# The last pass over each down weight piece on GpSimd instead of ScalarE

## The reference

```
scale = cond @ norm_w.T + 1.0
h = x * (scale[:, None, :] * rsqrt(mean(x * x, -1) + 1e-6))
val, gate = split(h @ up_w.T, 2, axis=-1)
h = val * gelu(gate)
hq = clip(round(h * s), -128, 127) / s        # s = 127 / max|h| of the token
wq = clip(round(down_w * t), -1, 1) / t       # t = 1 / mean|down_w|, one number for all
y = hq @ wq.T + x
```

## Time and profile before

| | |
|---|---|
| device time, median of 3 runs | 810.25 us (809.88 to 810.6) |
| profiled execution, its span (the page gives no other time of it) | 807.4 us |
| TensorE busy | 772.0 us, 96% |
| VectorE busy | 605.6 us, 75% |
| ScalarE busy | 443.2 us, 55% |
| GpSimd busy | 255.6 us, 32% |
| ScalarE's last pass over a down piece (L655), 8 times | 1.05 us each (median) |
| GpSimd's passes L527 and L530 over a down piece, 8 times each | 1.12 and 1.22 us each (medians) |

### The profile page before, as it was taken

One profiled execution on the slowest core, in us unless ns is written; L12 is line 12 of the kernel. 1 busy time (PEld: TensorE's weight loads), 2 busy tenths in 40 slices (PEclk: granted clock), 3 DMA queues, 4 the chain that ended last, 5 costly groups with the idle time before them and its releaser, 6 DMA issues.

```text
span 807.4 us, 18034 instructions
## 1 busy us (share of the span) xinstructions
PE 772.0 (96%) x6401; PEld 635.0 (79%) x6401; DVE 605.6 (75%) x852; ACT 443.2 (55%) x1025; POOL 255.6 (32%) x318
## 2 busy tenths in 40 slices
PE   5898988999799999999999999999999999999998
PEld 4687877788688877897788877898788877888753
DVE  5987987799568973899558973898558973887367
ACT  5687767587566643555446643555446643554323
POOL 3875966354422321123212321122212321111021
PEclk9999999999999999999999999999999999999999
DMA  5485764876465554654565554654565545555432
GB/s 207 169 264 170 239 226 175 309 243 218 160 223 198 185 187 148 223 206 145 188 213 200 184 169 151 230 203 140 193 219 195 182 162 162 188 187 175 133 126 83
DMA packets 37963, 152.90 MB, mean 189 GB/s; under 512 B 3608, under 2 KB 4128, under 8 KB 37920
## 3 DMA queue, kind: packets, MB, share of 16 engines
q1 hardware_dynamic: 37376, 152.06, 55.5%
q10 hardware_dynamic: 544, 0.27, 0.1%
HBM read 130.16 MB, written 22.15 MB: 189 GB/s over the span
## 4 chain that ended last, share of the span: by engine, by line
PE 71%; DVE 7%; DMA 1%; issue 1%; ACT 1%; SPq 0%; DVEq 0%; ACTq 0%
PE Y L1142 11%; PE A L1091 11%; PE A L1094 11%; PE A L1093 11%; PE B L1091 8%; PE B L1094 8%; PE B L1093 8%; DVE h L872 2%; DMA wslots<-w_scratch 1%; DVE h L838 1%; PE X L1039 1%; DVE h L832 1%; DVE mpart L851 1%; PE X L1131 1%; DVE q L877 1%
## 5 line engine op out<-in xcount | busy, mean ns | idle before, releaser
L1091 PE MATMUL A<-xT,wslots 128*128 (+1 forms) x1024 | 280.9, 274 | 13.4 <-ACT snapC L616 9.1
L1093 PE MATMUL A<-xT,wslots 128*128 (+1 forms) x1024 | 280.9, 274 | 0.0
L1094 PE MATMUL A<-xT,wslots 128*128 (+1 forms) x1024 | 280.9, 274 | 0.0
L509 POOL TENSOR_TENSOR snapC<-snapC 128x256 f32<-128x256 f32 x128 | 100.5, 785 | 503.4 <-ACT snapC L616 503.3
L1091 PE MATMUL B<-xT,wslots 128*128 (+1 forms) x768 | 210.4, 274 | 2.1 <-DVE h L832 2.1
L1093 PE MATMUL B<-xT,wslots 128*128 (+1 forms) x768 | 210.3, 274 | 0.0
L1094 PE MATMUL B<-xT,wslots 128*128 (+1 forms) x768 | 210.2, 274 | 0.0
L838 DVE SCALAR_TENSOR_TENSOR h<-h,c_all,g 128x512 f32<-128x512 f32 (+1 forms) x128 | 103.7, 810 | 111.0 <-ACT g L639 110.7
L1091 PEld LDWEIGHTS A<-xT,wslots 128*128 128x128 f16 x1024 | 100.7, 98 | 30.3 <-ACT snapC L616 11.0
L1093 PEld LDWEIGHTS A<-xT,wslots 128*128 128x128 f16 x1024 | 100.7, 98 | 14.6
L1094 PEld LDWEIGHTS A<-xT,wslots 128*128 128x128 f16 x1024 | 100.8, 98 | 12.2
(11 more groups left out here) (137 smaller groups left out, 944.0 us busy)
## 6 DMA issues: line engine op xcount, KB each, us to landing
wslots<-w_scratch SPq DMA_DIRECT2D x105, 896.0 KB, 4.6
w_scratch<-wslots SPq DMA_DIRECT2D x15, 896.0 KB, 5.2
wst<-in_L_cond_up_w_dram SPq DMA_DIRECT2D x16, 512.0 KB, 6.5
xin<-in_x_dram SPq DMA_DIRECT2D x8, 1024.0 KB, 7.5
dwb<-in_L_cond_down_w_dram SPq DMA_DIRECT2D x16, 512.0 KB, 4.4
wst<-in_x_dram SPq DMA_DIRECT2D x28, 256.0 KB, 5.3
out_dram<-wst SPq DMA_DIRECT2D x28, 256.0 KB, 2.1
xin<-in_x_dram SPq DMA_DIRECT2D x4, 256.0 KB, 4.1
```

Source lines behind the costliest of these rows:

```text
L509: pool.tensor_tensor(snapC[:, s % 2, 0:H], snapC[:, s % 2, 0:H], snapC[:, s % 2, H:T], ALU.add)\
L1091: pe.matmul(into, high, xh, start=(start and kp == 0), stop=False, skip_group_check=not start)
L1093: pe.matmul(into, high, xl, start=False, stop=False, skip_group_check=not start)
L1094: mm = pe.matmul(into, low, xh, start=False, stop=last, skip_group_check=not start)
```

## The change

GpSimd makes the third pass itself, right behind its second, in down_clip, with a tensor_scalar (subtract MAGIC, multiply by 1.0) that writes f16 into tern. The two waits of the pass go with it. ScalarE's down_round and its table of slots are gone. The signal dw_rounded now comes from GpSimd; the transposes of TensorE and the loads of SyncE wait for it as before, and stand where they stood.

```diff
--- before.py
+++ after.py
@@ -109,7 +109,6 @@
     PC = FF // 2
     DW_SUM = {2 * i: i for i in range(PIECES)}
     DW_CLIP = {s: i for i, s in enumerate((0, 2, 3, 5, 6, 9, 11, 13))}
-    DW_TERN = {s + 1: i for s, i in DW_CLIP.items()}
     DW_T = {s + 2: i for s, i in DW_CLIP.items()}
     DW_LOAD_WITH = {6: 3, 7: 4, 9: 5, 10: 6, 13: 7}
 
@@ -529,6 +528,10 @@
                 pool.wait_ge(dw_added, i + 1)
                 pool.tensor_scalar(dwb[:, i % 2, :], dwb[:, i % 2, :], MAGIC + 1.0, MAGIC - 1.0, ALU.min, ALU.max)\
                     .then_inc(dw_clipped, 1)
+                pool.wait_ge(dw_clipped, i + 1)
+                at_least(pool, dT_psum, i - 1)
+                pool.tensor_scalar(tern[:, i % 2, :], dwb[:, i % 2, :], MAGIC, 1.0, ALU.subtract, ALU.mult)\
+                    .then_inc(dw_rounded, 1)
 
             def batch(b, first=False, final=False):
                 for s in range(FT):
@@ -649,11 +652,6 @@
                 act.activation(q_of(LAST, i), h_tiles(LAST, 2 * PAIR_ORDER[i], 2), ACT.Copy, bias=-MAGIC)\
                     .then_inc(qe_rounded_act, 1)
 
-            def down_round(i):
-                act.wait_ge(dw_clipped, i + 1)
-                at_least(act, dT_psum, i - 1)
-                act.activation(tern[:, i % 2, :], dwb[:, i % 2, :], ACT.Copy, bias=-MAGIC).then_inc(dw_rounded, 1)
-
             def y_scale(t):
 
                 act.wait_ge(dq_ready, BEFORE + 1)
@@ -685,8 +683,6 @@
                     gelu_second(of, before)
                     if not final:
                         x_ahead(b + 1, s)
-                    if first and s in DW_TERN:
-                        down_round(DW_TERN[s])
                     if first and s in DW_T:
                         i = DW_T[s]
                         act.wait_ge(dT_psum, i + 1)
```

## The result

The changed kernel takes 814.28 us (median of 5 runs, 811.45 to 815.85) where the kernel before takes 810.25 us: a ratio of 1.0052, with a 95% interval of 1.0031 to 1.0073. The forecast was 810.6 us, with a range to 812.3. Run again on another chip, beside more runs of the kernel before, the ratio was 1.0040 (1.0026 to 1.0053). The change makes the kernel 0.4 to 0.5% slower.

A forecast was written before the change was run, and what follows sets the result against it. It took TensorE's wait in batch 1 behind VectorE's chain as the bound: -0.95 us from ScalarE's pass and +1.4 on the chain make the restart 0.4 us later, 810.25 + 0.4 = 810.6 us, range 809.2 to 812.3.

The forecast's parts named there:

- What bounds the kernel: Batch 1: TensorE stands still 7.1 us, 4.4 of it behind VectorE's chain and two ScalarE instructions; removing one gives -0.95 us.
- so I take 1.05 us: Each new GpSimd pass over 128x1024 was priced at 1.05 us from the clip pass, eight making 8.4 us.
- The prediction's own sign of being wrong: The forecast is wrong if the new GpSimd pass takes over 1.3 us.
- the bound set on the unknown: Price of shared access on VectorE's chain: no collision leaves -0.95 us, four at 0.86 leave +2.1.
- The collisions: VectorE's chain in batch 1 waits behind new GpSimd passes at pieces 2, 3 and 5; +1.4 us in sum.
- Elsewhere the next gate_second is a slot away, and TensorE waits for none of it: GpSimd's gate_second queued behind the new pass at pieces other than 0 costs TensorE nothing.
- Loads and transposes behind the pass: Transposes lie a slot behind, cost 0; SP's down-piece loads get free some microseconds sooner, counted 0.
- Rival E: An early down-piece load delays the weight slot TensorE waits for, by 1.24 us: 811.8 us; chance 0.05.
- The clock: Around TensorE's restart in batch 1 the half clock stays; restarting before the drop would return 1.4 us, 808.3; chance 0.06.
- Rival D: VectorE between 166 and 206: each of GpSimd's three passes holds one VectorE instruction, chain +3.1 us, 812.4 us; chance 0.12.

The follow-up runs named there:

- defer5: Kernel before, with ScalarE's last pass over piece 5 moved behind the three snap copies of slot 11; 808.91 us, ratio 0.9993.
- price: A kernel of its own timing GpSimd passes over 128x1024 by themselves, then VectorE instructions beside one; subtract took 3.63 us, add 1.04.
- add: Changed kernel with the third pass written as add -MAGIC instead of subtract MAGIC; 811.03 us, ratio 1.0016 to the kernel before.
- queue: Kernel before, ScalarE's pass kept, plus three 128x4 powers on GpSimd behind each clip pass; 812.09 us, ratio 1.0021.
- dummy: Kernel before, ScalarE's pass kept, plus an unused subtract pass on GpSimd behind each clip pass; 814.73 us, ratio 1.0076.
- inner: Kernel before with the changed subtract pass on GpSimd for pieces 1 to 5 alone, ScalarE keeping the others; 811.17 us, ratio 1.0007.
- inner2: Second run of inner, the subtract pass on GpSimd for pieces 1 to 5 alone, against the kernel before; 811.27 us, ratio 1.0015.
- norm2: defer5 with ScalarE normalising two of the four tiles of the next x in batch 1; 806.61 us, ratio 0.9954 to the kernel before.
- lockmap: A kernel of its own: four GpSimd passes (subtract, add, twice) beside rows of tiny VectorE instructions; the first beside the third pass took 0.99 us.

## Why the prediction was wrong

- **What bounds the kernel**: right. Of the batches from 1 on it is batch 1 in which TensorE loses time, behind VectorE's chain, and ScalarE's pass stood on the path for 0.95 us (defer5). In the changed kernel's first profile TensorE spent its waits inside the chain (1.7 and 3.3 us) and had none left at the restart; that VectorE's earlier wait would grow and be taken off the later one was said, that it would take all of it was not.
- **"so I take 1.05 us"**: the step that failed. The forecast took the pass from a clip pass (minimum and maximum) and one with multiplications, and asked only whether f16 output has a surcharge. It has none; the subtract has one, of 2.6 us for each piece (price: 3.63 us against 1.04). No tensor_scalar of GpSimd with a subtract stood in the trace, and the bound set on the unknown was a bound on collisions, not on the pass. The prediction's own sign of being wrong, a pass of over 1.3 us, is what came. With the pass at 1.05 us the rest of the working comes out (add: 811.03 us, ratio 1.0016, forecast 810.6); with the pass at 3.6 us it is 814.
- **The collisions**: right where the pass is short (add: 1.52 us at both L834 named, +1.5 on the chain for +1.4, and the split by piece as well). With the slow pass the chain gets +3.9, of which the one collision that was forecast and came, at 166.73, is 0.8.
- **"Elsewhere the next gate_second is a slot away, and TensorE waits for none of it"**: wrong for a pass of 3.6 us. Pass and clip passes take 6 us, more than a slot (5.5, a sixteenth of 88.79), so gate_second, the power and x_mix come late (queue: 2.1 us on the chain), and in one of the two profiles TensorE waited 1.8 us behind pieces 6 and 7.
- **Loads and transposes behind the pass**: no cost is seen (dummy, which leaves them as they were, costs as much as the change). Rival E falls: TensorE's wait for the weight slot did not grow, 1.0 us against 1.7.
- **The clock**: the forecast had one stretch of half clock, as before (3.4 us in all). The changed kernel's two profiles have one of 6.8 us in its place, and so have add, dummy and inner; inner2 has none. What decides that is not shown.
- **Rival D** had the sign and the engine, and its 812.4 is nearest, by luck: its mechanism, three holds in step at 1.05 us each, is not what happened.

The sum after the fact, an estimate: +3.9 on the chain (measured), -0.95 of ScalarE, 0 to 1.8 behind the restart at pieces 6 and 7, and more or less half clock: 3 to 5 us, where 3.6 and 4.0 were measured. How it is shared between the chain and the clock in the timed runs is not shown; that the slow pass is the cause is shown: add, which differs from the changed kernel in that one operation, ends x_low 2.4 us sooner and is 2 to 3 us faster by the ratios.

## What to carry to other kernels

A pass that moves to another engine is priced by a row with the same engine, the same form and the same operation; if the trace has none, it is measured by itself first or the range is opened to several times the nearest row. On GpSimd write x - c as x + (-c). And before a pass goes to the engine that shares VectorE's access, ask whether VectorE is the chain that TensorE waits for: here the move gave ScalarE back 8 us, of which 0.95 mattered, and cost VectorE's chain 1.5 us even with the fast pass, while norm2, which takes 1.35 us from that chain on top of defer5's 0.95, is 0.46% faster.

## What the runs showed of the hardware

- GpSimd's tensor_scalar (subtract, multiply) with two immediates: 3.63 us for 128x1024, f32 in, into f16 and f32 alike; with add, multiply or minimum in place of subtract, and for a cast into f16, 1.04 (price).
- That pass of 3.6 us holds up VectorE's instructions with two SBUF operands for its first 1.0 us only, and a tensor_scalar for its first and last 1.0 us (lockmap).
- Small VectorE instructions are held up as long as large ones: a 128x4 one of 0.16 us took 1.07, a 128x16 one 1.00.
- The granted clock's stretches at half speed differ between executions whose chains are alike: in batch 1, 6.8 us in both profiles of the changed kernel and in inner's, none in inner2's, where x_low is 58.2 to 58.3 us on in all four. Two profiles of one kernel have periods 1.6 us apart (changed, 90.89 and 92.50) and 2.8 apart (inner and inner2, 93.03 and 90.27), so one profile does not price a change of a microsecond or two.
